# Two attention layers: from a loop over pairs of head groups with K held twice to unrolled units, chunk by chunk, with four slots for q and K

## What is computed

```python
scores = jnp.einsum('bhqd,bhkd->bhqk', q, k) / jnp.sqrt(jnp.asarray(hd, x.dtype))
scores = jnp.where(causal, scores, jnp.asarray(-jnp.inf, x.dtype))
attn = jax.nn.softmax(scores, axis=-1)
y = jnp.einsum('bhqk,bhkd->bhqd', attn, v)
```

## Time and profile before

| | us |
|---|---|
| median of 3 runs (1092.42 to 1098.62) | 1092.92 |
| span of the profiled execution, first to last instruction | 1084.4 |
| attention 0, first maxima to last copy out | 150.8 to 471.5 |
| attention 1, first maxima to last copy out | 635.5 to 900.5 |

### The profile page before, as it was taken

How to read it: one execution, slowest core, us unless ns; L and a number is a source line. 1 busy time by engine, 2 the same in 40 slices (tenths; PEclk the granted TensorE clock), 3 DMA queues, 4 the chain that set the end, 5 groups by cost and what they waited for, 6 DMA issues and landing times. The chain is left out here.

```text
span 1084.4 us, 17334 instructions
## 1 busy us (share of the span) xinstructions
PE 924.4 (85%) x5462; PEld 512.0 (47%) x5462; DVE 700.9 (65%) x1305; ACT 485.7 (45%) x750; POOL 254.2 (23%) x397
## 2 busy tenths in 40 slices
PE   7879943789988898888977877999999988799998
PEld 5557821333333333257535532333444426677766
DVE  6975332668666766448584765988888835745564
ACT  4221401336544655642262213566666673346730
POOL 2554020022112111210614531221212223012300
PEclk9998965889889989999788977999999999999999
DMA  9221161112211321020001330011111101042001
GB/s 315 88 89 59 23 144 42 42 48 87 71 56 59 81 72 54 11 97 1 1 0 56 103 94 23 24 46 46 46 44 44 24 1 39 11 173 78 20 21 59
DMA packets 45537, 64.87 MB, mean 60 GB/s; under 512 B 9056, under 2 KB 32160, under 8 KB 43936
## 3 DMA queue, kind: packets, MB, share of 16 engines
q1 hardware_dynamic: 45472, 64.01, 19.7%
HBM read 51.27 MB, written 12.32 MB: 59 GB/s over the span
## 5 line engine op out<-in xcount | busy, mean ns | idle before, releaser
L1035 DVE TENSOR_REDUCE mx<-psum 128x1 f32<-128x512 f32 (+3 forms) x640 | 372.1, 632 | 157.9 <-PE psum L866 132.1
L980 ACT ACTIVATE arena_p<-psum 128x1024 f32<-128x1024 f32 (+3 forms) x384 | 294.0, 808 | 271.5 <-PE psum L883 270.7
L861 PE MATMUL psum<-arena_s 96*128 96x512 bf16 (+3 forms) x768 | 236.7, 349 | 53.8 <-DMA arena_s<-k_parts 43.4
L883 PE MATMUL psum<-arena_s 99*128 99x512 bf16 (+3 forms) x768 | 191.1, 340 | 30.3 <-DMA arena_s<-mT 26.7
L1098 POOL TENSOR_SCALAR_AFFINE_SELECT arena_p<-arena_p 128x256 f32<-128x256 f32 x256 | 102.8, 407 | 472.5 <-ACT arena_p L980 470.7
L903 PE MATMUL psum<-arena_p,v_grp 128*32 128x512 f32 (+3 forms) x1536 | 171.2, 519 | 2.1 <-POOL arena_p L1098 1.9
L861 PEld LDWEIGHTS psum<-arena_s 96*128 96x128 bf16 x768 | 77.5, 102 | 200.9 <-DVE mx L1035 107.4
L883 PEld LDWEIGHTS psum<-arena_s 99*128 99x128 bf16 x768 | 64.9, 100 | 94.9 <-ACT arena_p L980 23.4
L866 PE MATMUL psum<-maskb,ident_b 128*128 128x128 bf16 x512 | 109.1, 235 | 0.0
L255 PE MATMUL psum<-x_h,w 128*128 128x512 f32 x224 | 89.9, 465 | 10.4 <-DVE w L472 7.3
L866 PEld LDWEIGHTS psum<-maskb,ident_b 128*128 128x128 bf16 x512 | 54.1, 106 | 13.0 <-issue 1.6
(11 more groups left out here) (200 smaller groups left out, 1087.3 us busy)
## 6 DMA issues: line engine op xcount, KB each, us to landing
q_parts<-arena_p SPq DMA_DIRECT2D x48, 128.0 KB
arena_s<-q_parts SPq DMA_DIRECT2D x32, 192.0 KB, 3.0
arena_s<-k_parts SPq DMA_DIRECT2D x16, 384.0 KB
ff_raw<-in_w_in SPq DMA_DIRECT2D x11, 512.0 KB, 3.5
arena_s<-q_parts SPq DMA_DIRECT2D x32, 128.0 KB, 2.9
arena_s<-k_parts SPq DMA_DIRECT2D x16, 256.0 KB
k_parts<-arena_p SPq DMA_DIRECT2D x30, 128.0 KB
arena_w<-in_w SPq DMA_DIRECT2D x12, 256.0 KB, 6.5
```

The source lines that it names most:

```text
L861: last = pe.matmul(psum[:, bank, width * n:width * n + width], q_st[0:KS, s, c, 512 * r + P * i:512 * r + P * i + P], k_max[0:KS, s, T * k ...
L883: last = pe.matmul(psum[:, 2 * hp + h, o:512], k_exp[0:KM, s, T * kh + P * kt:T * kh + P * kt + P], q_st[0:KM, s, c, 512 * r + o:512 * r + ...
L980: act.activation(pr[:, n % NP_RING, :, o:512], psum[:, 2 * (b % 2):2 * (b % 2) + 2, o:512], ACT.Exp, scale=scale).then_inc(exp_ready, 1)
L1035: dve.tensor_reduce(mx[:, kc, col:col + 4 * len(heads) - 3:4], src, AX, ALU.max)\
```

## The change

- The hardware loop is gone: 16 units are written out per layer, with plain numbers for addresses and waits.
- The order of the units is chunk by chunk: the eight groups' chunk 0 (u = 0 to 7), then the eight groups' chunk 1 (u = 8 to 15).
- K is held once per unit and serves maxima and scores. q and K have four slots (`NS`); the load of unit u + 4 is issued when the last scores of unit u are done. Chunk 0 loads only the first 512 keys. In layer 0 these are six DMAs of 16 partitions instead of three; chunk 1 keeps the three of before.
- The maxima of up to three units ahead run beside a unit (`issued_by`): the entries of units 2 to 9 are spread evenly over units 0 to 7, those of unit u + 2 over unit u from 8 on, none beside units 14 and 15 save the last "T".
- Scores run two key tiles ahead of the values, exponentials go into a ring of eight (four of them in `arena_x`, where the transposed input stood), and two key tiles' values are issued near one another.
- The four small operations that cut the maxima go from DVE to POOL (`split_max`); DVE keeps the join of two halves for chunk 1. "T" stands at place 4 of the next unit's entries instead of 2.
- The store of the maxima is one DMA with 3 rows instead of three DMAs. `load_first` loads four units in layer 0 and two in layer 1. Four slots of -1 rows are set instead of two.

```diff
-NP_RING = 4
+NP_RING = 8
+NS = 4
...
+        self.q = view(arena_s, 0, [NS, R * 512], BF16)
+        self.k = view(arena_s, 16384, [NS, self.kr * T], BF16)
...
+    def load_k(self, sp, u):
+        c, g = divmod(u, NG)
+        dst = self.k[:, u % NS, :].rearrange("p (h t) -> p h t", t=T)
+        for kp, copies in enumerate(((0, 1, 2), (3, 4), (5,))):
+            heads = self.k_parts[kp, :, self.kr * g:self.kr * g + self.kr, :]
+            if c == 1 or self.kr == 1:
+                n, t = len(copies), 512 * (c + 1)
+                sp.dma_start(dst[D * copies[0]:D * (copies[0] + n), :, 0:t].rearrange("p h t -> p (h t)"),
+                             heads[:, :, 0:t].rearrange("(o d) h t -> o d (h t)", o=1)
+                             .broadcast_to([n, D, self.kr * t])).then_inc(self.k_loaded[u % NS], 16)
+                continue
+            for j in copies:
+                sp.dma_start(dst[D * j:D * j + D, :, 0:512], heads[:, :, 0:512])\
+                    .then_inc(self.k_loaded[u % NS], 16)
...
+    steps = [(c, g) for c in range(CH) for g in range(NG)]
+    TURN_AT = 4
...
+    def issued_by(u, slot):
+        def goal(u):
+            if u >= NG:
+                return first_entry[min(u + 2, NU + 1)]
+            return first_entry[2] + (first_entry[NG + 2] - first_entry[2]) * u // NG
+        if u >= NU - 2:
+            return first_entry[NU + 1]
+        return goal(u) + (goal(u + 1) - goal(u)) * slot // (4 * n_tiles[steps[u][0]])
...
+            def load_max(u):
+                s = u % NS
+                sp.wait_ge(qk_taken, turn_entry(u) + 1)
+                sp.dma_start(q_st[KS:KM, s, :].rearrange("j (a q) -> j a q", q=P), mT[:, u % 2, :])\
+                    .then_inc(max_loaded[s], 16)
...
+            for u in range(stacked.first, NS):
+                stacked.load(sp, u)
+            load_max(0)
+            for u in range(NU):
+                if u + 1 < NU:
+                    load_max(u + 1)
+                if u + NS < NU:
+                    sp.wait_ge(scores_ready, first_exp[u + 1])
+                    stacked.load(sp, u + NS)
...
+                at = blocks.index((u, 0))
+                for n in range(0, n_tiles[c], 2):
+                    ahead = blocks[at + n + 2:at + n + 4]
+                    for k, (au, akt) in enumerate(ahead):
+                        for p in range(2 - k):
+                            scores(au, akt, p)
+                            maxima(4 * n + 2 * k + p + 1)
+                    values(u, n)
+                    maxima(4 * n + 5)
+                    values(u, n + 1)
+                    maxima(4 * n + 7)
+                    if ahead:
+                        scores(*ahead[1], 1)
+                    maxima(4 * n + 8)
...
+            def split_max(u):
+                s, c = u % 2, steps[u][0]
+                m, (high, mid, low) = mx[:, s, 0, :], [mst[:, s, j, :] for j in range(NPART)]
+                if c == 1:
+                    pool.wait_ge(max_joined, u - NG + 1)
+                else:
+                    pool.wait_ge(qk_taken, first_entry[u] + len(lists[u]))
+                if u >= 2:
+                    pool.wait_ge(qk_ready, turn_entry(u - 2) + 1)
+                pool.tensor_copy(high, m).then_inc(max_high, 1)
...
+            for u, (c, g) in enumerate(steps):
+                for b in range(2 * n_tiles[c]):
+                    while split < NU and first_entry[split + 1] <= issued_by(u, max(0, 2 * b - 4)):
+                        split_max(split)
+                        split += 1
...
+                if u + 2 < NU:
+                    load_v(u + 2)
```

More of the change, by code:

```diff
@@ new lines, in k_count, with load, load_first, first @@
+    def k_count(self, u):
+        return sum(96 if self.kr == R and v < NG else 48 for v in range(u % NS, u + 1, NS))
+    def load(self, sp, u):
+        self.load_q(sp, u)
+        self.load_k(sp, u)
+    def load_first(self, sp):
+        for u in range(self.first):
+            self.load(sp, u)
+    @property
+    def first(self):
+        return NS if self.kr == R else 2
+def attention(nc, layer, phase, stacked, arena_o, arena_p, arena_x, v_tok, v_grp, ident_b, maskb,
+              psum):
+    q_st, k_st, q_loaded, k_loaded, kr = stacked.q, stacked.k, stacked.q_loaded, stacked.k_loaded, stacked.kr
@@ new lines, in pieces, with entries @@
+    def pieces(u):
+        c = steps[u][0]
+        out = []
+        for i in range(4):
+            for kc in range(c):
+                out += [(i, (r,), kc, 512) for r in range(R)]
+            heads = [(0, 1), (2, 3)] if i < 2 else [(r,) for r in range(R)]
+            out += [(i, hs, c, P * (i + 1)) for hs in heads]
+        return out
+    def entries(b):
+        out = pieces(b) if b < NU else []
+        if b >= 1:
+            out.insert(min(TURN_AT, len(out)), "T")
+        return out
```

433 lines of the change are left out of this document (150 added, 283 removed).

## The result

The changed kernel takes 1107.69 us (median of four runs, 1102.99 to 1114.69), the kernel before 1094.91 in the same session (1092.42 to 1098.62). The ratio is 1.013 with a 95% interval of 1.008 to 1.019: slower by 1.3%, where 1051 was forecast, and above the whole range (1018 to 1083).

What follows compares the result with a forecast made beforehand. Attention 1 was taken as bound by PE's own matmuls, attention 0 by those plus transfers. Gains of 12.5 (start), 22.6 (body 0) and 6.6 (attention 1) sum to 41.7: 1092.9 - 41.7 = 1051, range 1018 to 1083.

Steps and rivals of the forecast that it cites:

- steady units: Both attentions: PE's work per unit unchanged; chunk 1 units with 29 entries take 20.0 us, chunk 0 units 10.2.
- the first: Rival for the units: they run at DVE's pace or better, 30 us less, 1021; chance 0.17.
- forecast bodies: First scores to the end of each attention: 266.8 us in attention 0, 241.5 in attention 1.
- Waits of attention 0: PE waits for K loads and stored maxima around units 6 to 9 of attention 0: sum 31 us.
- The second rival: Attention 0, units 9 to 14: maxima stores behind K each wait some 5 us, 30 more, 1081; chance 0.12.
- Start of attention 0: Before attention 0's first scores: they come at 169.6 instead of 182.06, 12.5 us gained.
- Attention 1's start: Ahead of attention 1: SP's loads for a second unit make the phase start 3.4 us later.
- Units 14 and 15: Last two units of each layer, without entries: 15 us each and 1.2 for the tail, 31.2.
- The third rival: Both attentions: POOL becomes late and PE stands at every "T", 58 us more, 1109, slower; chance 0.05.
- the 8.5 us that the prediction took to lie around the span: Whole kernel before: median 1092.92 us against span 1084.4; trace differences were subtracted from 1092.9.

Runs made afterwards that it cites:

- e1: Changed kernel with PE handling one key tile at a time again, scores still two tiles ahead: 1046.2 us, ratio 0.957.
- e8: Changed kernel going tile by tile, chunk 1 K loads of layer 0 in six DMAs, units alternating between chunks: 1095.1 us, ratio 1.003.
- e9: Changed kernel with each block's scores shared out, two pairs, both value tiles, two pairs: 1081.6 us, ratio 0.989.

## Why the prediction was wrong

The step that failed is the one on steady units: "PE's work per unit is unchanged", and from it "A chunk 1 unit with 29 entries beside it takes ... 20.0 us" and 10.2 for a chunk 0 unit. PE's work was unchanged. Its pace was not, since I took the pace from an order of scores, one pair to a slot, that the change does away with. I had read in the new order that two entries stand between the value tiles, and used it only to strike a gain; I did not lay the same order against ACT, which had 10 of 29 us free on average and so looked harmless. The average hides that every pair of scores has to wait for an exponential two pairs back. That waits could grow here stood in none of the rivals; the first had it the other way round, with the two tiles ahead closing gaps.

Its size: forecast bodies 266.8 and 241.5 us, measured 301.6 and 269.7, 35 and 28 too long. What the runs showed in place of 20.0 and 10.2 us is 22.85 for a chunk 1 unit and 10.7 to 12.1 for a chunk 0 unit without a long wait. With the block alone undone the bodies are 269.4 and 241.6, within 2.6 and 0.1 us of the forecast, and the time is 1046 against a forecast of 1051. So the rest of the sum held, by its parts:

- **Waits of attention 0.** Unit 7 1.46 us (2.8 forecast), unit 8 15.83 (14.5), unit 9 7.61 (7.4), unit 8's maxima 6.61 (6.2), and none for K from unit 10 on. Right in place and size. The second rival, a store behind K in each chunk 1 unit, did not come.
- **Start of attention 0.** POOL's rows to 161.95, the split done at 163.76 (164.5 forecast), first scores 167.72 (169.6). Right.
- **Attention 1's start.** From the end of attention 0 to the first scores 181.1 us, 177.5 before: 3.6 later, 3.4 forecast. Right.
- **Units 14 and 15.** 15 us each and a tail were forecast. In e1's last stretch of 75.8 us two units with entries take 40.3 and two tiles of unit 11 some 5, which leaves 30.5: right. With the block the same stretch is 10.9 us longer, of which the two units with entries have 5.4.
- **The third rival.** It was the only one on the slower side, and its 1109 us came near the measured time by luck alone. In the changed kernel PE waits for POOL 9.6 us in attention 0, 7.4 of them once at the start. e8 shows that it decides in another order of units.

The sum of the misses, from the profiled runs: -1.9 at the first start, +34.8 and +28.2 in the bodies, +0.6 for the second start and the tail, and -6.8 for the 8.5 us that the prediction took to lie around the span, where 1.7 do here. That is +55, and 1051 + 55 is the profiled 1106. The last term hid part of the miss: taken from span to span the forecast was 1084.4 - 41.7 = 1042.7, and the changed kernel's span is 1104.5, 62 us above it (e1's is 1043.9).

The order rows shown ahead of the prediction had it: in rows 715 to 720 four score matmuls in two pairs, with one entry between them, each pair waiting for `exp_ready`. What was left out is a count between pairs. A pair of scores can only start when the pair two ahead is computed and its exponential over, 0.6 + 0.95 = 1.55 us after that one's start at the least; PE got there after 1.5 in the run above (822.06 to 823.77, less the wait), and sustained runs need 0.95 a pair where PE takes 0.6 and an entry. On the other side, if ACT is not to run dry, no stretch without scores may be longer than the two exponentials that two pairs of banks can hold for it, 1.9 us; the block has 3.2. Of the two, the first weighs more here: e9 still has stretches of 2.5 us and more without scores, and its score matmuls start only 0.5 us late in a unit.

A rule of the Trainium skill points the same way (Perfetto Trace Analysis, Optimization Strategy): consistent bubbles, the same gap in each repetition on the engine that should be saturated, can mean too few buffers for the next tile. The 48 short waits of the changed kernel are such bubbles, and there are just two pairs of banks; but e1 has only 8 and 7 of them in the two attentions with the same two pairs, by the order alone.

## What to carry to other kernels

Where one engine feeds another through two buffers, take the order in which it writes them as a cost of its own: no engine's busy share shows it, and runs on one side must be no longer than what the buffers and the partner's time allow. Before gathering like instructions into runs, weigh what a run saves (here 0.4 us a unit) against what it does to the spacing (here 2.7). And when a change brings a new form of a transfer along with a new structure, try the form alone in the old structure first: here six DMAs for three gave the old kernel 65 us, and the new structure with the same six DMAs and its block undone (e5) nothing more that could be measured.

## What was not expected of the hardware

- The form of a DMA decided between 49 and 216 GB/s for the same 768 KB, and that alone was 6% of the kernel's time.
- Of the 2.7 us that the block costs a unit, only 1.8 can be seen as idle time; the other 0.9 is in PE's modelled busy time (21.04 against 20.15 us with the same instructions, both at full clock). Counted from start to start, all of the 2.7 stands ahead of score matmuls. At 823.16 an entry is modelled with 0.38 us and the scores behind it start at 823.77, a wait of 0.23; in e1 scores follow such an entry after 0.22 (737.10 and 737.32), so that the wait cost 0.39. Waits too short to show as idle are hidden in the same way: e9's unit has 0.27 us idle and is 1.0 longer than e1's.
- With equal instructions in attention 1, e5's chunk 0 units ran at a mean granted clock of 0.94 and took 86.5 us, e1's at 0.98 and 84.4; both are means of stretches at full clock (2.4 GHz) and short ones at half. Why the two differ is open.
